# Cross attention: the reciprocals of the softmax sums move from GpSimd to VectorE in the six steps whose probabilities GpSimd normalises

## The reference

```python
q = (query @ Wq + bq).reshape(b, sq, N_HEAD, KEY_DIM)
k = (key @ Wk + bk).reshape(b, key.shape[1], N_HEAD, KEY_DIM)
v = (value @ Wv + bv).reshape(b, value.shape[1], N_HEAD, VALUE_DIM)
scores = jnp.einsum('bqhd,bkhd->bhqk', q, k) / TEMP
attn = jax.nn.softmax(scores, axis=-1)
out = jnp.einsum('bhqk,bkhd->bqhd', attn, v).reshape(b, sq, N_HEAD * VALUE_DIM)
out = out @ Wo + bo + residual
```

## Time and profile before

| | |
|---|---|
| median of three runs | 2169.98 us (2169.52 to 2170.1) |
| the profiled execution | 2167.39 us, its span 2165.3 us |
| mean granted TensorE clock | 0.994 |
| TensorE busy | 2105.9 us, 97% |
| VectorE busy | 1568.3 us, 72% |
| ScalarE busy | 1274.7 us, 59% |
| GpSimd busy | 942.2 us, 44% |
| POOL rinv (L436) | 96 of 1008 ns, 96.8 us |
| POOL probs (L439) | 96 of 1895 ns, 182.0 us |
| DVE rinv (L710), steps 0 and 7 | 32 of 178 ns |

### The profile page before, as it was taken

One profiled execution on the slowest core, in us unless ns is written; L12 is line 12 of the kernel. 1 busy time (PEld: TensorE's weight loads), 2 busy tenths in 40 slices (PEclk: granted clock), 3 DMA queues, 4 the chain that ended last, 5 costly groups with the idle time before them and its releaser, 6 DMA issues.

```text
span 2165.3 us, 46201 instructions
## 1 busy us (share of the span) xinstructions
PE 2105.9 (97%) x15864; PEld 1848.8 (85%) x15865; DVE 1568.3 (72%) x2774; ACT 1274.7 (59%) x3067; POOL 942.2 (44%) x786
## 2 busy tenths in 40 slices
PE   8999999999999999999999999899998999999997
PEld 7898888888888888888988888677776888888886
DVE  7667767767677677677677676688886887666665
ACT  5565666655665665666566566477775335555553
POOL 5223322332333333224223332388884334777775
PEclk9999999999999999999999999999999999999999
DMA  5000000010010000000100100244542222333332
GB/s 154 11 21 25 15 29 24 10 34 19 15 34 15 19 25 23 19 24 10 34 19 15 34 10 1 63 158 153 153 126 96 88 79 54 55 54 52 56 53 42
DMA packets 100685, 103.90 MB, mean 48 GB/s; under 512 B 11952, under 2 KB 90160, under 8 KB 100624
## 3 DMA queue, kind: packets, MB, share of 16 engines
q1 hardware_dynamic: 86992, 84.47, 12.6%
q0 software_dynamic: 13632, 18.62, 5.3%
HBM read 72.52 MB, written 30.54 MB: 48 GB/s over the span
## 4 chain that ended last, share of the span: by engine, by line
PE 64%; DVE 12%; POOL 9%; issue 7%; ACT 5%; DMA 2%; POOLq 0%; DVEq 0%; ACTq 0%
PE banks L915 32%; PE banks L958 6%; PE banks L1016 5%; PE banks L988 5%; POOL out_dram L2406 4%; PE banks L1647 3%; POOL r_x L2370 3%; PE banks L1003 3%; DVE q_st L658 2%; DVE top L678 2%; DVE peak L675 2%; PE banks L2245 2%; DMA out_dram<-r_y,index 2%; POOL index L2377 2%; ACT probs L547 1%
## 5 line engine op out<-in xcount | busy, mean ns | idle before, releaser
L915 PE MATMUL banks<-ctxT_hi,qk_hi 128*128 128x256 f32 x1024 | 301.2, 294 | 0.0
L915 PE MATMUL banks<-ctxT_hi,qk_lo 128*128 128x256 f32 x1024 | 290.1, 283 | 0.0
L915 PE MATMUL banks<-ctxT_lo,qk_hi 128*128 128x256 f32 x1024 | 287.8, 281 | 0.0
L547 ACT ACTIVATE probs<-banks,nbias 128x256 f32<-128x256 f32 x512 | 236.6, 485 | 85.1 <-DVE nbias L680 84.7
L436 POOL TENSOR_TENSOR rinv<-rsum,inverse 128x4 f32<-128x4 f32 x96 | 96.8, 1008 | 409.4 <-ACT probs L547 409.4
L554 ACT ACTIVATE pc<-banks 128x512 f32<-128x512 f32 x256 | 153.3, 599 | 189.2 <-PE banks L915 186.1
L638 DVE TENSOR_TENSOR qk_lo<-banks,qk_hi 128x512 fp32r<-128x512 f32 x256 | 163.8, 686 | 87.5 <-ACT qk_hi L509 87.5
L675 DVE TENSOR_REDUCE peak<-banks 128x4 f32<-128x1024 f32 x128 | 156.4, 1222 | 91.1 <-PE banks L915 90.9
L638 DVE TENSOR_TENSOR pT_lo<-banks,pT_hi 128x512 fp32r<-128x512 f32 x256 | 165.7, 685 | 56.5 <-ACT pT_hi L509 55.9
L915 PE MATMUL banks<-pT_hi,ctx_hi 128*128 128x512 f32 x512 | 204.6, 400 | 1.7 <-DVE pT_lo L638 1.7
L915 PE MATMUL banks<-pT_hi,ctx_lo 128*128 128x512 f32 x512 | 202.1, 395 | 0.0
(11 more groups left out here) (271 smaller groups left out, 6170.2 us busy)
## 6 DMA issues: line engine op xcount, KB each, us to landing
ctx_raw<-in_ctx_dram SPq DMA_DIRECT2D x64, 256.0 KB, 2.7
experts_w<-in_L_ffn_We_dram SPq DMA_DIRECT2D x24, 512.0 KB, 3.9
x_in<-in_x_dram SPq DMA_DIRECT2D x16, 256.0 KB, 2.7
x_again<-in_x_dram SPq DMA_DIRECT2D x16, 256.0 KB, 2.8
x_stream<-z SPq DMA_DIRECT2D x16, 256.0 KB, 2.1
s_x<-x_stream SPq DMA_DIRECT2D x32, 128.0 KB, 3.8
s_x_again<-x_stream SPq DMA_DIRECT2D x32, 128.0 KB, 2.8
x_normalised<-s_xl SPq DMA_DIRECT2D x32, 128.0 KB, 1.7
```

Of the source, the lines that this page charges most:

```text
L547: nc.scalar.activation(probs[:, s % 2, p, :], scores[:, s % 2, p // 2, (p % 2) * SK:(p % 2 + 1) * SK], ACT.Exp, bias=nbias[:, s % 2, p:p + ...
L915: last = nc.tensor.matmul(out, a, b, start=(n == 0), stop=(n == 3 * len(pairs) - 1))
```

## The change

In steps 1 to 6 the reciprocal of the sums is now VectorE's, as in steps 0 and 7; GpSimd waits for it and does the product alone. VectorE's reciprocal stands at the end of its step, behind pT_lo and, in step 4, ahead of the two additions for resid. `inverse` and its memset go, and the setup semaphore is waited for at 2 instead of 3. In the new file `resid<-xln,bo` is L891, the reciprocal L885, `peak` L670, `top` L673, `nbias` L675, L638 is L633, and the product L434.

```diff
-    inverse = sb("inverse", [P, PAIRS])
...
-        nc.gpsimd.memset(inverse[:, :], -1.0).then_inc(pool_setup, 1)
...
-        pool.wait_ge(pool_setup, 3)
+        pool.wait_ge(pool_setup, 2)
...
         def normalise(g, s):
-            pool.wait_ge(exp_done, PAIRS * (STEPS * g.at + s + 1))
-            pool.sem_inc(pool_past, 1)
-            nc.gpsimd.tensor_tensor(rinv[:, s % 2, :], rsum[:, s % 2, :], inverse[:, :], ALU.pow).then_inc(rinv_done, 1)
             pool.wait_ge(rinv_done, len(POOL_STEPS) * g.at + s)
             pool.sem_inc(pool_past, 1)
...
                 if g.cur and s not in POOL_STEPS:
                     normalise(g, s)
+                if g.cur and s in POOL_STEPS:
+                    dve.wait_ge(exp_done, PAIRS * (STEPS * g.at + s + 1))
+                    nc.vector.reciprocal(rinv[:, s % 2, :], rsum[:, s % 2, :]).then_inc(rinv_done, 1)
...
-        pe.wait_ge(pool_setup, 3)
+        pe.wait_ge(pool_setup, 2)
```

## The result

| | median of the runs | lowest to highest | runs |
|---|---|---|---|
| before, beside it | 2169.75 us | 2168.93 to 2170.66 | 8 |
| after | 2176.06 us | 2173.66 to 2179.49 | 8 |

The ratio is 1.0027, its 95% interval 1.0018 to 1.0037: the changed kernel is slower by 6.3 us, where 7.9 were forecast. The profiled execution took 2173.66 us, its span 2171.9.

A forecast was written before the change was run, and what follows sets the result against it. TensorE was taken as the bound (busy 580.71 of 583 us), not GpSimd or VectorE. +10.8 - 2.0 - 0.9 = +7.9 us took the median from 2169.98 to 2177.9 us; range 2159 to 2184.

The forecast's parts named there:

- The cost at step 5: Transposes of step 5: step 4's second resid addition waits for GpSimd's product, ctxT_lo comes late; 0.72 us times 15 groups, 10.8 us.
- the faster rival: Step 4: both resid additions slip in ahead of the product, step 5's 0.43 us go; -9.4 us, 2160.6 us, chance 0.25.
- Step 2: Transposes of step 2: step 1's product starts about 1.0 us earlier; gain 0.13 us a group, 2.0 us in 15 groups.
- Group 0: First group: TensorE waits openly for step 1's chain; gain 0.9 us, bounds 0 and 1.0.
- Steps 3 and 6: Product waits for VectorE's queued reciprocal but stays covered by TensorE's work; ctx halves move behind the product in step 6; zero.
- The last group: Transposes of step 5: waits for GpSimd's product taken as hidden, so its earlier start there counted as zero.
- The clock rival: Step 5: the longer gap drops TensorE's clock to 1.2 GHz for eight transposes; 15.5 us, 2193 us or more, chance 0.03.
- Two inputs in SBUF: VectorE instructions with both inputs in SBUF, such as `top` and the resid additions, wait behind GpSimd's; those reading PSUM don't.

The follow-up runs named there:

- product_at_0_32: The changed kernel with a GpSimd memset of 128x40 between its wait and the product of step 4: 2175.31 us, ratio 1.0029.
- product_later: The changed kernel with a GpSimd memset of 128x256 between its wait and the product of step 4: 2158.26 us, ratio 0.9941.
- step4_alone: The kernel before with the reciprocal moved to VectorE in step 4 only, powers left on GpSimd in the other steps: 2178.05 us, ratio 1.0045.
- recip_behind_resid: The changed kernel with VectorE's reciprocal of step 4 placed behind the two additions for resid instead of ahead: 2156.78 us, ratio 0.9944.
- one_input_same_length: The changed kernel with resid made from xln minus and plus a number of its row, one large SBUF input, bo left out: 2173.84 us, ratio 1.0018.
- additions_later: The changed kernel with one more VectorE instruction on SBUF data between the reciprocal of step 4 and the additions for resid: 2179.03 us, ratio 1.0044.

## Why the prediction was right, and where it wasn't

**The cost at step 5 (+0.72 us a group forecast, 0.66 measured).** Counted from the end of the exponentials (672.46 in the chain above, where the first piece starts 0.03 later), the steps came out as worked out: the reciprocal after 0.03 us (0.03 said), the first addition after 0.13 (0.15), the product after 0.38 (0.39), `peak` after 2.51 (2.58), the end of ctxT_lo after 4.74 (4.82). The lead of the product over the second addition was 0.342 - 0.254 = 0.088 us (0.09 said). The handoff times and the pair z and L424 in the earlier trace rows carried over almost unchanged. It was close, though: with some 0.07 us more on GpSimd (0.088 - 0.016) the faster rival would have been the result; 0.06 more did not do it (product_at_0_32), 0.25 more did (product_later). The chance of 0.25 for it was not too large.

**Step 2 (-0.13 forecast).** The longest distance among the transposes of step 2 went from 0.33 to 0.20 us, 0.13 us, as in the transposes of step 6, which stayed at 0.20.

**Group 0 (-0.9 forecast, about -2.1 measured): the term came true, and something else came on top.** The group took 85.79 us instead of 87.25, and its step 5 lost 0.64 more (1.07 for 0.43), so the rest gained 1.46 + 0.64 = 2.1. From its first transposes of probs to the second it is 10.87 us instead of 11.73: 0.86 gained, the forecast term. From the second to the third it is 17.15 instead of 18.37: 1.22 us that I had not forecast. The wait at the transposes of step 2 shrank as I took it, from 2.19 to 1.30 us; before, then after:

```profile
48.76 0.63 PE L988 MATMUL banks<-ident,probs 128*128 128x128 f32 x4 [2.19 <-DVE q_st L658]
```

```profile
48.20 0.63 PE L986 MATMUL banks<-ident,probs 128*128 128x128 f32 x4 [1.30 <-DVE q_st L653]
```

In the 1.22 us TensorE's clock differs. Windows (length; busy PE, PEld, DVE, ACT, POOL; granted clock; DMA share, GB/s), before and after:

```profile
49.60:56.50 6.90, 6.02 (x29) 6.03 (x30) 2.21 (x4) 1.98 (x4) 0.00 (x0) 0.51 0.00 0
56.50:63.00 6.50, 4.45 (x26) 3.73 (x26) 3.57 (x7) 4.49 (x13) 2.37 (x2) 1.00 0.00 0
63.00:67.00 4.00, 4.00 (x19) 3.76 (x18) 1.72 (x3) 1.96 (x4) 0.54 (x1) 0.57 0.00 0
```

```profile
49.60:56.50 6.90, 6.59 (x41) 6.42 (x42) 3.27 (x7) 1.46 (x4) 1.90 (x1) 0.76 0.00 0
56.50:63.00 6.50, 4.42 (x17) 3.65 (x16) 2.67 (x4) 4.44 (x13) 0.00 (x0) 0.75 0.00 0
63.00:67.00 4.00, 3.92 (x31) 3.57 (x31) 2.50 (x5) 3.55 (x7) 0.00 (x0) 0.98 0.00 0
```

Before, 6.90 us went by at about half of full speed (1.2 GHz) right behind the long wait, and most of 4.00 us more; in full-speed time the three windows hold 6.90 x 0.51 + 6.50 + 4.00 x 0.57 = 12.3 us. After, they hold 6.90 x 0.76 + 6.50 x 0.75 + 4.00 x 0.98 = 14.0 us. The 1.7 us between them cover the 1.22; part of them is time in which TensorE waits, so they are an upper bound.

The shorter wait is not needed for this. In step4_alone nothing is changed up to step 4, and the wait is still 2.18 us; yet from the second to the third transposes it takes 17.16 us like after, and windows of the same lengths have a granted clock of 0.75, 0.79 and 0.91, 13.9 us in full-speed time (wait, then the first window):

```profile
49.14 0.63 PE L992 MATMUL banks<-ident,probs 128*128 128x128 f32 x4 [2.18 <-DVE q_st L659]
```

```profile
50.00:56.90 6.90, 6.04 (x38) 6.00 (x39) 3.30 (x5) 1.96 (x4) 0.00 (x0) 0.75 0.00 0
```

In the traces of all the other kernels that stretch took 15.95 to 17.47 us; the kernel before, of which there is one trace, has the longest. So the clock in group 0 differs from trace to trace, and no run shows that any of the 1.22 us belongs to the change.

**Steps 3 and 6 (zero forecast).** In step 3 the product ends at 666.80 (664.90 + 1.90) and the transposes that need it start at 668.85: 2.05 us of cover, where I had counted on 0.92, since the reciprocal found a place right behind pT_lo. The distances within the transposes of step 6 are those of before, 0.20 us.

**The last group (-0.13 forecast, -0.60 measured): a term that was put at nothing.** The prediction calls all 16 waits for GpSimd's product hidden, and counts the gain of an earlier product at step 5 as zero. The last group transposes no next context, and there the transposes of step 5 waited openly for it (before; the product runs from 1348.54 to 1350.44):

```profile
1350.49 1.10 PE L988 MATMUL banks<-ident,probs 128*128 128x128 f32 x8 [0.26 <-POOL probs L439]
```

With the product 1.0 us earlier the wait is gone: from the transposes of step 4 to these it is 6.49 us instead of 6.91, 0.42 us gained.

**The sum.** From the first to the last transpose of probs the traces show +5.35 us: +7.41 for the 14 inner groups together (14 x (0.66 - 0.13) makes 7.42), -1.46 for group 0, -0.60 for the last. Of the inner groups twelve grew by 0.50 us each, the two behind group 0 by 0.75 and 0.66; why those two did is open. The medians differ by 6.3 us; the span by 6.6. Of the -1.46, 1.22 are the stretch with the other clock, which is not shown to be the change's; without it the traces would differ by some 6.6 us, as an estimate (5.35 + 1.22).

**The clock rival (0.03).** It did not come: the steady stretch of after, with 1.12 us of loss in each group, has a granted clock of 1.00 as in the earlier trace rows.

**The faster rival (2160.6 us forecast).** Its mechanism and its size can be read off the runs in which the additions do go first: 2156.8 to 2159.7 us. `top` waits 0.5 us and the loss at step 5 goes, as described; a group falls from 84.65 to 84.09 us, 0.56, where 0.43 + 0.13 were forecast. It was 1 to 4 us short, and 1.25 of that are group 0 again (84.67 for 87.25 us in recip_behind_resid, -2.6, where 0.43 + 0.9 were forecast), in the same stretch as above (17.05 for 18.37).

**Two inputs in SBUF.** The prediction gives this as what the waiting instructions have in common. It is too narrow: one_input_same_length was held as well. The forecast did not hang on it.

A held product takes h - 0.140 us more, never the whole of h, and so does a held addition. The second addition of after starts 1.837 us before the product ends and takes 2.118 us, where 0.420 + 1.837 would be 2.257: 0.139 less. In product_at_0_32 it is 1.865 us before, and 2.145 instead of 2.285. The Trainium skill (SBUF — State Buffer, "Who interferes with whom") lets the later one block fully until the holder is done; the additions and products held here lie 0.14 us below that, on both sides (a product with h under 0.140 us, by h). By its rule the product of an inner group of after would have taken 1.893 + 0.172 = 2.065 us, as an estimate; it took 1.925. The prediction says that the trace agrees for VectorE. That is right for the order and not for the length: z ended 0.29 us after L424, less than the 0.476 us of its shortest. The same section of the Trainium skill lists `tensor_scalar` among the forms that can take the shared port, which the run with one input bears out and my reading of the earlier trace rows did not.

## What to carry to other kernels

Before an instruction with a wait is put into a queue, look at what stands behind it and needs no wait: if that can go first, into the time in which the engine waits anyway, put it first; here that was worth 18.9 us for the same instructions. When work moves from one of two engines that take turns at SBUF to the other, lay out who starts when to 0.05 us; a freed microsecond on an engine that nobody waits for can bring its next instruction into the way of one that somebody waits for. And treat such an order as fragile: where the turn is 0.09 us away, enforce it by the order of the queue and don't leave it to the durations.

## What the runs showed of the hardware

- VectorE's additions with both inputs in SBUF, and its TENSOR_SCALAR from SBUF to SBUF, take turns with GpSimd's product by single instructions. `peak` (PSUM to SBUF) and BATCH_NORM_STATS2 (SBUF to SBUF) do not: they keep their 1.22 and 0.42 us inside a GpSimd product. Between two of VectorE's additions the product had its turn with 0.028 us of lead or more and not with 0.016 or less; in additions_later 0.035 were not enough. An addition of 0.42 us that loses its turn lasts 2.12 us and ends 0.28 us after the product.
- Its busy time is no work: of VectorE's 2.46 us for resid in a group of after, 1.71 are waiting, and no view calls it so. The sign is an instruction whose least and greatest length lie far apart.
- A GpSimd product is held only for what goes beyond its first 0.140 us (the table above, six cases to within 3 ns), and VectorE's addition likewise (2.118 and 2.145 us for 2.257 and 2.285).
- A memset of 98 ns, 131 ns and 312 ns for 1, 40 and 256 columns moves the next GpSimd instruction by 0.034, 0.060 and 0.247 us. A delay of 0.06 us turned the order in the first and last group alone and left the time where it was (2175.31 us), one of 0.25 us turned it everywhere and was worth 17.4 us.
